# A recurrent scan over 128 steps: exponentials issued a step ahead, expert tiles spread over three steps, and four extra bf16 matrices ahead of each step's spreads

## The chip, the cores and the metric

The kernel runs on one core of a Trainium2 chip. The metric is the time of the whole program on the device in microseconds, as the median over several runs. One core has five engines that run their own instruction streams and meet only at semaphores: TensorE (PE in the profile, with its weight loads as PEld), VectorE (DVE), ScalarE (ACT), GpSimd (POOL) and SyncE (SP), which here only issues DMAs.

## The reference: what is computed

The network has four layers over 4096 tokens of 128 channels. Every layer normalises x, computes a mixer s and a feed-forward part g, and adds s * silu(g) to x. The change lies in layer 2, whose mixer is a selective scan (Mamba) and whose feed-forward part picks 2 of 16 experts for each token:

```python
xz = xn @ W_in;  xi, z = split(xz)
xc = silu(causal_conv(xi) + conv_b)
dt_lo, Bm, Cm = split(xc @ W_xp)
delta = softplus(dt_lo @ W_dt + dt_bias);  A = -exp(A_log)
def step(h, inp):                        # 256 channels x 16 states
    dA = exp(dt_t[..., None] * A)
    h = h * dA + (dt_t * u_t)[..., None] * B_t[:, None, :]
    return h, einsum('bdn,bn->bd', h, C_t)
y = (ys + xc * D_skip) * silu(z);  s = y @ W_out + x

h = relu(tensor @ W1[e] + b1[e]);  y = h @ W2[e] + b2[e]   # experts, 512 hidden
```

Each of 16 sequences has 256 tokens; the reference writes the layers for smaller batches and the kernel applies them to all.

## The kernel before, in words

Layers 0 and 1 run first in one loop over 8 chunks of 512 tokens (two sequences), then `layer2_route` normalises, routes the tokens to experts and scatters them into sorted rows, then `layer2_mix` does the scan and the experts, then layer 3 runs in a loop. Only `layer2_mix` and the layout of one weight array are touched.

`layer2_mix` is written out without a loop: CHUNKS = 8 chunks of 512 tokens, each with PAIRS = 16 steps, 128 steps in all. With k the chunk, n the step in it and g = 16k + n, one step handles 16 of the 256 inner channels as two groups of 8 channels x 16 states, so each group fills 128 partitions. What a step does:

- PE `spread_pairs` (L1094): four fp32 matrices of 32 rows by 512 columns. Two copy the rows of delta (`DL`) for step g + 1 into banks 0 and 1 of the PSUM, two copy delta * u (`DU`) for step g into banks 2 and 3. It waits for ACT's exponentials of step g (`decay_ready`), which read banks 0 and 1, and for DVE's product of step g - 1 (`drive_done`), which reads banks 2 and 3. The four lie on different rows of the array and run together; an fp32 matrix is two instructions in the trace.
- ACT `decay` (L1253): two exponentials, `DA`, double buffered.
- DVE `drive`: the product with B (L1337, `DB`), then the scan over time (L1343, `ST`).
- POOL (L1398): the product with C.
- PE `add_states` (L1122), every second step: sums over the 16 states.

Beside this, two kinds of work are cut into pieces and attached to steps. `head(k + 1, n)` is one of up to 16 pieces of the next chunk's preparation (layer norm, input projection, convolution, silu, softplus), on PE, ACT and DVE; all PE pieces go through the one PSUM bank `LANE`, so a PE piece waits for the ACT copy of the piece before it. Piece 7 holds both silus with a table load on either side, piece 11 the first part of the softplus, piece 12 its logarithm, again with two table loads. And each chunk has 10 expert tiles of 128 rows (SLOTS), from step FIRST = 5 on: `tile_rows` transposes the rows on PE (L1140), ACT copies them (L1262, `XT`); `tile_hidden` is the first expert matrix on PE (L1145) and four relus on ACT (L1267, `H`); `tile_out` is the second matrix with its bias on PE (L1156, L1157) and a copy on ACT (L1274, `YO`). Step n does rows and hidden of tile j and the output of tile j - 1.

The order on each engine is the order in which the code is written. ACT's order in a step is decay(n), XT, YO, H, head piece n; PE's is spreads, rows, output of j - 1, hidden of j, states, head piece n. SP loads each tile's weights as one transfer of 578 KB, `WB`, and its rows, `XR`, once the output of the tile two before has been computed.

Of the kernel before, what the change touches and what calls it, by code (L numbers as in the profile page):

```python
# [12 lines left out]
D = 128  # L13
# [962 lines left out]
MIX_SEMS = (LN_SEMS + LINKS + "xn_loaded0 xn_loaded1 xn_loaded2 s_stored tile_loaded0 tile_loaded1 tile_stored0 tile_stored1 rows_ready rows_taken hid_ready hid_done out_ready out_taken "  # L976
# [4 lines left out]
FIRST = 5  # L981
PAIRS = DI // 16
RING = 4


def layer2_mix(nc, c, w, wf, r, xn_mid, s_mid, xs_mid, ys_mid, PB):
    with ExitStack() as ctx:
# [5 lines left out]
        xn_loaded, tile_loaded, tile_stored = (s.xn_loaded0, s.xn_loaded1, s.xn_loaded2), (s.tile_loaded0, s.tile_loaded1), (s.tile_stored0, s.tile_stored1)  # L993
        B1 = 2 * HID2
        B2 = B1 + 4
# [5 lines left out]
        with nc.Block() as block:  # L1001
            @block.sync
            def _(sp):
# [38 lines left out]
            def _(pe):  # L1042
# [54 lines left out]
                def spread_pairs(k, n):  # L1097
# [35 lines left out]
                def tile_rows(j):  # L1133
                    k = j // SLOTS
                    pe.wait_ge(tile_loaded[j % 2], 32 * (j // 2 + 1))
# [12 lines left out]
                def tile_out(j):  # L1148
                    k = j // SLOTS
                    pe.wait_ge(s.hid_done, 4 * j + 4)  # L1150
                    if j:
                        pe.wait_ge(s.out_taken, j)
                    if j % SLOTS == 0 and k + 1 < CHUNKS:
                        pe.wait_ge(s.xm_ready, k + 2)
                    for i in range(4):
                        nc.tensor.matmul(PB[:, SMALL, 0:128], b.H[:, i, :], b.WB[:, j % 2, HID2 + i * 128:HID2 + (i + 1) * 128], start=i == 0, stop=False)  # L1156
# [29 lines left out]
            def _(act):  # L1186
# [58 lines left out]
                def decay(k, n):  # L1245
                    g = PAIRS * k + n
                    h, i, strip = place(n)
# [10 lines left out]
                def tile_rows(j):  # L1258
# [3 lines left out]
                    nc.scalar.activation(b.XT[:], PB[:, WORK, 0:128], ACT.Copy).then_inc(s.rows_taken, 1)  # L1262
# [13 lines left out]
                for step in range(PAIRS):  # L1276
                    head(0, step)
                for k in range(CHUNKS):
                    for n in range(PAIRS):
                        decay(k, n)  # L1280
                        j = SLOTS * k + n - FIRST
                        if FIRST <= n < FIRST + SLOTS:
                            tile_rows(j)
                        if FIRST < n <= FIRST + SLOTS:
                            tile_out(j - 1)
                        if FIRST <= n < FIRST + SLOTS:
                            tile_hidden(j)
# [760 lines left out]
def layouts(i):  # L2048
# [22 lines left out]
    w2f = np.concatenate([i["L2_ffn_W1"], i["L2_ffn_W2"].reshape(E2, 4, 128, D).transpose(0, 2, 1, 3).reshape(E2, 128, 512),  # L2071
                          i["L2_ffn_b1"].reshape(E2, 4, 128).transpose(0, 2, 1), b2], 2)
# [40 lines left out]
```

## Time and profile before

| what | value |
|---|---|
| median of 3 runs | 4766.21 us (4755.93 to 4780.89) |
| profiled execution, its own time | 4755.87 us |
| its span | 4754.3 us |
| span, granted TensorE clock (mean) | 0.788 |
| PE busy, DVE busy, ACT busy, POOL busy | 3385.2, 2565.2, 1804.2, 1275.9 us |
| steps of `layer2_mix` in the trace | from 1356 to 2450 us |

Busy times are for the whole program; for the change only the stretch of `layer2_mix` counts, some 1090 us of the 4754. In the trace a step begins with the product on DVE (L1337), so the start of one to the start of the next is the length of a step. The granted clock is a share of full speed: 0.5 is 1.2 GHz and 1.0 is 2.4 GHz, and a mean in between says how the stretch was divided between the two. The start to start distances of the 8 chunks are 135.6, 144.4, 139.0, 140.9, 138.9, 140.0 and 144.4 us for chunks 0 to 6, and 96.1 us for the last, which has no next chunk to prepare; its steps 6 to 13 take 61.4 us of that. The page gives 3.4 us from issue to landing for a tile's weights and 3.6 us for its rows (medians of 80 each).

### The profile page before, as it was taken

What the parts mean: (1) busy time and instruction counts of PE and PEld (TensorE: products, weight loads), DVE (VectorE), ACT (ScalarE), POOL (GpSimd) and SP (SyncE); (2) the same over time, 40 slices, a digit from 0 to 9 for tenths busy, and PEclk for the clock granted to TensorE, in tenths of its full rate; (3) what the DMA queues carried; (4) which work ended last, traced back from release to release, by engine and by line L of the source; (5) the groups of instructions that cost most, each with busy time, mean ns of one, the idle gap of its engine ahead of it and who ended that gap; (6) DMA issues with size and microseconds to landing.
All of it is one profiled execution on the core that took longest, in us unless ns stands there. A gap on an engine that the chain in (4) does not pass through costs nothing. (4 is left out here: it accounts for less than half of the span.)

```text
span 4754.3 us, 51362 instructions
## 1 busy us (share of the span) xinstructions
PE 3385.2 (71%) x18378; PEld 1798.5 (38%) x18378; DVE 2565.2 (54%) x3680; ACT 1804.2 (38%) x3620; POOL 1275.9 (27%) x991
## 2 busy tenths in 40 slices
PE   6888888882357666666667868687686777868677
PEld 3444444441223333333333434343343433434343
DVE  3444444443645455555546656665565656656665
ACT  3333333332233343333323434344343443434344
POOL 0000000003412222322225334242442425334242
PEclk8888888885566676767677979888786887968888
DMA  1000000002211221111120000000000000000000
GB/s 81 7 7 7 7 7 7 7 7 89 74 33 49 66 64 50 60 53 47 54 68 1 5 8 5 8 2 6 5 5 8 5 8 1 5 8 5 8 2 6
DMA packets 70675, 111.70 MB, mean 23 GB/s; under 512 B 8640, under 2 KB 46016, under 8 KB 69952
## 3 DMA queue, kind: packets, MB, share of 16 engines
q1 hardware_dynamic: 65088, 97.85, 6.4%
q0 software_dynamic: 5376, 11.02, 0.9%
q8 instruction: 135, 2.21, 0.2%
q14 instruction: 76, 0.62, 0.0%
HBM read 82.09 MB, written 26.74 MB: 23 GB/s over the span
## 5 line engine op out<-in xcount | busy, mean ns | idle before, releaser
L1398 POOL TENSOR_TENSOR l_ST<-l_ST,l_CT 128x1024 f32<-128x1024 f32 x128 | 303.9, 2375 | 770.0 <-DVE l_ST L1343 770.0
L369 ACT ACTIVATE l_PT<-PB 128x512 f32<-128x512 f32 x512 | 277.9, 594 | 521.2 <-PE PB L280 521.2
L280 PE MATMUL PB<-l_QM,l_KP 32*128 32x256 f32 x2048 | 356.3, 476 | 131.7 <-DVE l_QM L418 76.0
L1094 PE MATMUL PB<-l_DL,consts 32*128 32x512 f32 x512 | 219.7, 938 | 311.3 <-ACT l_DA L1253 297.1
L1337 DVE TENSOR_TENSOR l_DB<-PB,l_BT 128x1024 f32<-128x1024 f32 x128 | 156.5, 1223 | 413.7 <-PE PB L1094 413.7
L407 DVE TENSOR_REDUCE keep_MXP<-PB 128x4 f32<-128x1024 f32 x256 | 301.3, 1218 | 109.8 <-PE PB L253 109.7
L280 PEld LDWEIGHTS PB<-l_QM,l_KP 32*128 32x128 f32 x2048 | 231.5, 233 | 246.6 <-ACT l_PT L369 98.0
L1343 DVE TENSOR_TENSOR_SCAN l_ST<-l_DA,l_DB 128x1024 f32<-128x1024 f32 x128 | 299.4, 2339 | 4.4
L1548 POOL TENSOR_TENSOR l_PT<-l_PT,l_PEN 128x512 f32<-128x512 f32 x168 | 213.4, 1292 | 157.9 <-ACT l_PT L369 157.9
L703 POOL MEMSET l_KV<- 128x4 f32 x8 | 0.8, 105 | 923.0 <-POOLq L109 923.0
L1812 POOL TENSOR_TENSOR l3f_SQ<-l3f_RW 128x512 f32<-128x512 f32 x128 | 147.1, 1149 | 312.7 <-ACT l3f_RW L1678 312.7
L1616 PE MATMUL PB<-l3f_QK 64*64 64x128 f32 x2048 | 168.7, 314 | 80.4 <-DVE l3f_QK L1752 80.4
L1094 PE MATMUL PB<-l_DU,consts 32*128 32x512 f32 x512 | 217.9, 936 | 0.0
L1094 PEld LDWEIGHTS PB<-l_DL,consts 32*128 32x128 f32 x512 | 52.7, 243 | 432.3 <-ACT l_DA L1253 430.1
L253 PE MATMUL PB<-l_KP,l_QP 32*128 32x256 f32 x2048 | 198.6, 516 | 15.6 <-issue 15.6
L1703 ACT ACTIVATE l3f_PP<-PB,l3f_MN 128x128 f32<-128x128 f32 x512 | 146.3, 368 | 163.7 <-DVE l3f_MN L1764 163.7
L1821 POOL TENSOR_TENSOR l3f_PP<-l3f_PP,l3f_RS 128x512 f32<-128x512 f32 x128 | 133.3, 1041 | 257.1 <-DVE l3f_RS L1770 257.1
L294 PE MATMUL PB<-l_PT,keep_VT 128*32 128x256 f32 x2048 | 161.4, 469 | 36.2 <-POOL l_PT L1548 25.6
L1616 PEld LDWEIGHTS PB<-l3f_QK 64*64 64x64 f32 x2048 | 134.4, 157 | 115.0 <-issue 111.8
L1817 POOL TENSOR_TENSOR l3f_C<-l3f_C 128x512 f32<-128x512 f32 x128 | 162.3, 1268 | 48.3 <-DVE l3f_C L1741 48.3
L1253 ACT ACTIVATE l_DA<-PB,keep_aneg 128x510 f32<-128x510 f32 x256 | 161.6, 688 | 33.9 <-PE PB L1094 24.6
L1584 PE MATMUL PB<-l3f_HS,w3fs 128*128 128x512 f32 x256 | 145.9, 654 | 37.1 <-DVE l3f_HS L1720 37.1
(414 smaller groups left out, 7327.6 us busy)
## 6 DMA issues: line engine op xcount, KB each, us to landing
l_WB<-in_w2f_dram SPq DMA_DIRECT2D x80, 578.0 KB, 3.4
l_XR<-xs_mid SPq DMA_DIRECT2D x80, 64.0 KB, 3.6
ys_mid<-l_YO SPq DMA_DIRECT2D x80, 64.0 KB, 3.4
s_mid<-keep_S SPq DMA_DIRECT2D x17, 256.0 KB, 2.0
w3fs<-in_w3f_dram SPq DMA_DIRECT2D x1, 3125.0 KB, 17.3
keep_XI<-in_x_dram SPq DMA_DIRECT2D x9, 256.0 KB, 3.2
x_mid<-keep_X SPq DMA_DIRECT2D x9, 256.0 KB, 3.2
keep_SI<-s_mid SPq DMA_DIRECT2D x9, 256.0 KB, 2.7
```

The lines of the kernel that those rows point to most:

```text
L253: last = nc.tensor.matmul(PB[:, r, qt * SEQ:(qt + 1) * SEQ], b.QP[rows, a, q0:q0 + 128], b.KP[rows, a, i, sq * SEQ:(sq + 1) * SEQ], start= ...
L280: last = nc.tensor.matmul(PB[:, 4 + u % STBANKS, kt * SEQ:(kt + 1) * SEQ], b.KP[rows, a, i, k0:k0 + 128], b.QM[rows, n % 2, :], start=True ...
L294: last = nc.tensor.matmul(PB[32 * r:32 * r + 32, 7, 0:SEQ], VT[:, 2 * sq + kt, 8 * a + 2 * r + i, :], b.PT[:, (NR * (2 * j + i) + r) % PSL ...
L369: nc.scalar.activation(b.PT[:, u % PSLOTS].rearrange("p k q -> p (k q)"), PB[:, 4 + u % STBANKS, :], ACT.Exp).then_inc(s.exp_done, 1)
L407: nc.vector.tensor_reduce(dst[:, 2 * pair:2 * pair + 2, :, 16 + n % 2], PB[:, 2 * pair:2 * pair + 2, :].rearrange("p r (t k) -> p r t k", ...
L1094: return nc.tensor.matmul(PB[:, bank + e, :], c.rowsel[q:q + 32, i * 128:(i + 1) * 128], src[q:q + 32, k % 2, h, :], start=True, stop=True)
L1253: last = nc.scalar.activation(b.DA[:, g % 2, e, :].rearrange("p (s t) -> p s t", t=SEQ)[:, :, 1:SEQ], PB[:, e, :].rearrange("p (s t) -> p ...
L1343: nc.vector.tensor_tensor_scan(b.ST[:, g % RING].rearrange("p k t -> p (k t)"), b.DA[:, g % 2].rearrange("p k t -> p (k t)"), b.DB[:, g % ...
L1398: nc.gpsimd.tensor_tensor(b.ST[:, g % RING], b.ST[:, g % RING], b.CT[:, k % 2, :].unsqueeze(1).broadcast_to([128, 2, T]), ALU.mult).then_i ...
L1548: nc.gpsimd.tensor_tensor(pt, pt, b.PEN[:, 2 * sq:2 * sq + 2, :], ALU.mult).then_inc(s.weighed_pool, 1)
L1616: nc.tensor.matmul(PB[r, k, win * 128:win * 128 + 2 * WIN], b.QK[r, hp, q0:q0 + WIN], b.QK[r, NT + hp, k0:k0 + 2 * WIN], start=win == 0, s ...
L1817: nc.gpsimd.tensor_tensor(b.C1[:, v % 2, :], b.C1[:, v % 2, :], b.C2[:, v % 2, :], ALU.add).then_inc(s.rot_summed, 1)
```

## The change

Four things change in `layer2_mix`.

1. ACT issues `decay(g + 1)` in step g instead of `decay(g)`, behind the output copy of a tile and ahead of the head piece and the relus. ACT's head pieces come one step later (piece n - 1 in step n), and so do DVE's pieces 11 and 12 of the softplus (now 12 and 13).
2. A tile now lies over three steps: rows of j, hidden of j - 1, output of j - 2, in the order output, hidden, states, rows on PE; FIRST is 4 instead of 5. The transposed rows go to the bank `SMALL`, which the outputs also use, instead of `WORK`.
3. Before each step's spreads, behind their waits, PE runs FILL = 4 bf16 matrices of 128 x 512 on constants into a bank that the spreads then overwrite. Their result is not used.
4. SP loads a tile in three transfers (rows, first matrix with its bias, second matrix with its bias), each with its own wait, and the weight array is laid out so that each part is contiguous.

```diff
-FIRST = 5
+FIRST = 4
+FILL = 4
@@ load_tile (SP)
+                    if j >= 2:
+                        sp.wait_ge(s.rows_ready, j - 1)
+                    sp.dma_start(b.XR[:, j % 2, :], xs_mid[bass.ds(row, 128), :]).then_inc(rows_loaded[j % 2], 16)
+                    matrices = wf[bass.ds(bank, 1), :, :].rearrange("e p f -> p (e f)")
+                    if j >= 2:
+                        sp.wait_ge(s.hid_done, 4 * (j - 1))
+                    sp.dma_start(b.WB[:, j % 2, 0:V2], matrices[:, 0:V2]).then_inc(first_loaded[j % 2], 16)
+                    if j >= 2:
+                        sp.wait_ge(s.out_ready, j - 1)
+                    sp.dma_start(b.WB[:, j % 2, V2:W2ROW], matrices[:, V2:W2ROW]).then_inc(second_loaded[j % 2], 16)
@@ spread_pairs (PE), behind its waits
+                    for _ in range(FILL):
+                        nc.tensor.matmul(PB[:, PAIR0, :], c.identb, c.windowb, start=True, stop=True)
@@ the pieces of a step (PE)
-                        if FIRST <= n < FIRST + SLOTS:
-                            tile_rows(j)
-                        if FIRST < n <= FIRST + SLOTS:
-                            tile_out(j - 1)
-                        if FIRST <= n < FIRST + SLOTS:
-                            tile_hidden(j)
+                        if FIRST + 2 <= n < FIRST + 2 + SLOTS:
+                            tile_out(j - 2)
+                        if FIRST + 1 <= n < FIRST + 1 + SLOTS:
+                            tile_hidden(j - 1)
...
+                        if FIRST <= n < FIRST + SLOTS:
+                            tile_rows(j)
@@ the pieces of a step (ACT)
+                decay(0)
                 for k in range(CHUNKS):
                     for n in range(PAIRS):
-                        decay(k, n)
                         j = SLOTS * k + n - FIRST
+                        if FIRST + 2 <= n < FIRST + 2 + SLOTS:
+                            tile_out(j - 2)
+                        if PAIRS * k + n + 1 < PAIRS * CHUNKS:
+                            decay(PAIRS * k + n + 1)
+                        if n and k + 1 < CHUNKS:
+                            head(k + 1, n - 1)
+                        if FIRST + 1 <= n < FIRST + 1 + SLOTS:
+                            tile_hidden(j - 1)
                         if FIRST <= n < FIRST + SLOTS:
                             tile_rows(j)
-                        if FIRST < n <= FIRST + SLOTS:
-                            tile_out(j - 1)
-                        if FIRST <= n < FIRST + SLOTS:
-                            tile_hidden(j)
-                        if k + 1 < CHUNKS:
-                            head(k + 1, n)
```

How this stands on the engines. First PE, a step in the middle of a chunk's tiles with one head piece (step 6 of a chunk). Before:

```order
L1094 MATMUL PB<-l_DL,consts 128x512
L1094 MATMUL PB<-l_DU,consts 128x512
L1094 MATMUL PB<-l_DL,consts 128x512
L1094 MATMUL PB<-l_DU,consts 128x512
L1140 MATMUL PB<-consts,l_XR 128x128
L1156 MATMUL PB<-l_WB,l_H 128x128 x4
L1157 MATMUL PB<-l_WB,consts 128x128
L1145 MATMUL PB<-l_XT,l_WB 128x128 x4
L1068 MATMUL PB<-l_XM,w2s 128x512
```

Spreads, rows (L1140), output of the tile before (L1156, L1157), hidden (L1145), head piece (L1068). The same step after:

```order
L1119 MATMUL PB<-windowb,identb 128x512 x4
L1103 MATMUL PB<-l_DL,consts 128x512
L1103 MATMUL PB<-l_DU,consts 128x512
L1103 MATMUL PB<-l_DL,consts 128x512
L1103 MATMUL PB<-l_DU,consts 128x512
L1173 MATMUL PB<-l_WB,l_H 128x128 x4
L1174 MATMUL PB<-l_WB,consts 128x128
L1162 MATMUL PB<-l_XT,l_WB 128x128 x4
L1151 MATMUL PB<-consts,l_XR 128x128
L1077 MATMUL PB<-l_XM,w2s 128x512
```

Four matrices on constants (L1119) stand ahead of the spreads, and the rows (L1151) have moved behind output and hidden. Second ACT, where the two silus are: steps 7 and 8 of a chunk before.

```order
L1253 ACTIVATE l_DA<-PB,keep_aneg 128x2x255 x2
L1262 ACTIVATE l_XT<-PB 128x128
L1274 ACTIVATE l_YO<-PB 128x128
L1267 ACTIVATE l_H<-PB,l_WB 128x128 x4
L1215 ACT_TABLE_LOAD
L1215 ACTIVATE l_ZS<-l_ZS 128x1024
L1218 ACTIVATE l_XC<-l_XC 128x512 x2
L1219 ACT_TABLE_LOAD
L1253 ACTIVATE l_DA<-PB,keep_aneg 128x2x255 x2
L1262 ACTIVATE l_XT<-PB 128x128
```

The exponentials of step 8 (the second L1253 row) stand behind the silus and their table loads. After, step 8 of a chunk and the start of step 9:

```order
L1290 ACTIVATE l_YO<-PB 128x128
L1269 ACTIVATE l_DA<-PB,keep_aneg 128x2x255 x2
L1232 ACT_TABLE_LOAD
L1232 ACTIVATE l_ZS<-l_ZS 128x1024
L1235 ACTIVATE l_XC<-l_XC 128x512 x2
L1236 ACT_TABLE_LOAD
L1283 ACTIVATE l_H<-PB,l_WB 128x128 x4
L1278 ACTIVATE l_XT<-PB 128x128
L1290 ACTIVATE l_YO<-PB 128x128
L1269 ACTIVATE l_DA<-PB,keep_aneg 128x2x255 x2
```

The exponentials of step 9 (the first L1269 row) now stand ahead of the silus, and the relus and the copy of the rows (L1283, L1278) behind them.

## Rows read from the trace of the kernel before

**Rows 1.** Stretches by engine: busy us (count) of PE, PEld, DVE, ACT, POOL, clock, DMA.
```profile
1782.10:1923.00 140.90, 98.10 (x411) 47.08 (x410) 76.89 (x52) 54.58 (x115) 41.21 (x18) 0.69 0.19 56
...
2346.30:2442.40 96.10, 67.86 (x356) 35.37 (x356) 61.06 (x34) 33.22 (x88) 33.26 (x16) 0.79 0.24 70
```

**Rows 2.** Waits summed over 1365 to 2445 us: us, times, longest.
```profile
PE PB L1094 <- ACT l_DA L1253: 296.3, 113, 6.4
...
PEld PB L1140 <- DMA l_XR<-xs_mid: 36.4, 26, 1.9
```

**Rows 3.** Timeline, DVE products, chunk 3: start us, us, engine, line, operation, idle before.
```profile
1782.06 1.23 DVE L1337 TENSOR_TENSOR l_DB<-PB,l_BT 128x1024 f32<-128x1024 f32 x1 [1.16 <-PE PB L1094]
...
1826.32 1.22 DVE L1337 TENSOR_TENSOR l_DB<-PB,l_BT 128x1024 f32<-128x1024 f32 x1
...
1832.26 1.22 DVE L1337 TENSOR_TENSOR l_DB<-PB,l_BT 128x1024 f32<-128x1024 f32 x1 [2.40 <-PE PB L1094]
...
1846.54 1.23 DVE L1337 TENSOR_TENSOR l_DB<-PB,l_BT 128x1024 f32<-128x1024 f32 x1 [10.73 <-PE PB L1094]
...
1864.87 1.22 DVE L1337 TENSOR_TENSOR l_DB<-PB,l_BT 128x1024 f32<-128x1024 f32 x1 [5.47 <-PE PB L1094]
...
1872.59 1.23 DVE L1337 TENSOR_TENSOR l_DB<-PB,l_BT 128x1024 f32<-128x1024 f32 x1 [3.53 <-PE PB L1094]
...
1885.33 1.23 DVE L1337 TENSOR_TENSOR l_DB<-PB,l_BT 128x1024 f32<-128x1024 f32 x1 [2.25 <-PE PB L1094]
...
1909.04 1.22 DVE L1337 TENSOR_TENSOR l_DB<-PB,l_BT 128x1024 f32<-128x1024 f32 x1 [7.69 <-PE PB L1094]
...
1923.01 1.22 DVE L1337 TENSOR_TENSOR l_DB<-PB,l_BT 128x1024 f32<-128x1024 f32 x1 [2.12 <-PE PB L1094]
```

**Rows 4.** Timeline of PE, chunk 3, at the lower clock.
```profile
1844.23 1.22 PE L1094 MATMUL PB<-l_DL,consts 32*128 32x512 f32 x1 [5.49 <-ACT l_DA L1253]
...
1846.52 1.91 PE L1156 MATMUL PB<-l_WB,l_H 128*128 128x128 f32 x8
...
1834.80 2.08 PE L1145 MATMUL PB<-l_XT,l_WB 128*128 128x128 f32 x8
...
1836.81 1.94 PE L1122 MATMUL PB<-l_ST,consts 128*32 128x512 f32 x8
```

**Rows 5.** Timeline of PE, chunk 3, at the higher clock.
```profile
1863.52 0.69 PE L1094 MATMUL PB<-l_DL,consts 32*128 32x512 f32 x1 [1.83 <-ACT l_DA L1253]
...
1864.75 1.06 PE L1156 MATMUL PB<-l_WB,l_H 128*128 128x128 f32 x8
...
1866.15 1.16 PE L1145 MATMUL PB<-l_XT,l_WB 128*128 128x128 f32 x8
...
1867.24 1.12 PE L1081 MATMUL PB<-l_BC,w2s 32*128 32x512 f32 x2
```

**Rows 6.** Timeline of PE, eight bf16 matrices on constants (layer 3), both clocks.
```profile
2477.95 3.56 PE L127 MATMUL PB<-windowb,identb 128*128 128x512 bf16 x8
...
2646.71 1.89 PE L127 MATMUL PB<-windowb,identb 128*128 128x512 bf16 x8
```

**Rows 7.** Timeline of ACT, chunk 3.
```profile
1834.91 0.28 ACT L1274 ACTIVATE l_YO<-PB 128x128 f32<-128x128 f32 x1 [1.94 <-PE PB L1157]
...
1836.91 1.14 ACT L1267 ACTIVATE l_H<-PB,l_WB 128x128 f32<-128x128 f32 x4 [1.73 <-PE PB L1145]
...
1838.08 1.28 ACT L1215 ACT_TABLE_LOAD   x1
...
1842.92 1.26 ACT L1253 ACTIVATE l_DA<-PB,keep_aneg 128x510 f32<-128x510 f32 x2
...
1890.03 1.28 ACT L1233 ACT_TABLE_LOAD   x1
...
1893.69 0.60 ACT L1240 ACTIVATE l_BT<-PB 128x512 f32<-128x512 f32 x1
```

**Rows 8.** Groups by line, 1365 to 2445 us: busy us, mean ns | idle before.
```profile
L1343 DVE TENSOR_TENSOR_SCAN l_ST<-l_DA,l_DB 128x1024 f32<-128x1024 f32 x128 | 299.4, 2339 | 4.4
```

More of the change, by code:

```diff
@@ L992, in layer2_mix @@
         SO = c.S
-        xn_loaded, tile_loaded, tile_stored = (s.xn_loaded0, s.xn_loaded1, s.xn_loaded2), (s.tile_loaded0, s.tile_loaded1), (s.tile_stored0, s.tile_stored1)
-        B1 = 2 * HID2
-        B2 = B1 + 4
+        xn_loaded, tile_stored = (s.xn_loaded0, s.xn_loaded1, s.xn_loaded2), (s.tile_stored0, s.tile_stored1)
+        rows_loaded, first_loaded, second_loaded = (s.rows_loaded0, s.rows_loaded1), (s.first_loaded0, s.first_loaded1), (s.second_loaded0, s.second_loaded1)
+        B1 = HID2
+        V2 = B1 + 4
+        B2 = V2 + HID2
         PAIR0, WORK, SMALL, LANE, SUMS = 2, 5, 6, 7, 4
@@ L1134, in tile_rows, with tile_hidden @@
                     k = j // SLOTS
-                    pe.wait_ge(tile_loaded[j % 2], 32 * (j // 2 + 1))
+                    pe.wait_ge(rows_loaded[j % 2], 16 * (j // 2 + 1))
+                    if j >= 2:
+                        pe.wait_ge(s.out_taken, j - 1)
+                    if j % SLOTS == 0 and k + 1 < CHUNKS:
+                        pe.wait_ge(s.xm_ready, k + 2)
+                    nc.tensor.transpose(PB[:, SMALL, 0:128], b.XR[:, j % 2, :], c.ident).then_inc(s.rows_ready, 1)
+                def tile_hidden(j):
+                    k = j // SLOTS
+                    pe.wait_ge(s.rows_taken, j + 1)
+                    pe.wait_ge(first_loaded[j % 2], 16 * (j // 2 + 1))
                     if j:
@@ L1148, in tile_out @@
                 def tile_out(j):
-                    k = j // SLOTS
                     pe.wait_ge(s.hid_done, 4 * j + 4)
+                    pe.wait_ge(second_loaded[j % 2], 16 * (j // 2 + 1))
+                    if j % SLOTS < SLOTS - 1:
+                        pe.wait_ge(s.rows_taken, j + 2)
                     if j:
                         pe.wait_ge(s.out_taken, j)
-                    if j % SLOTS == 0 and k + 1 < CHUNKS:
-                        pe.wait_ge(s.xm_ready, k + 2)
                     for i in range(4):
-                        nc.tensor.matmul(PB[:, SMALL, 0:128], b.H[:, i, :], b.WB[:, j % 2, HID2 + i * 128:HID2 + (i + 1) * 128], start=i == 0, stop=False)
+                        nc.tensor.matmul(PB[:, SMALL, 0:128], b.H[:, i, :], b.WB[:, j % 2, V2 + i * 128:V2 + (i + 1) * 128], start=i == 0, stop=False)
                     nc.tensor.matmul(PB[:, SMALL, 0:128], c.ones[0:1, :], b.WB[0:1, j % 2, B2:B2 + 128], start=False, stop=True).then_inc(s.out_ready, 1)
@@ L1243, in head, with decay @@
                         nc.scalar.activation(b.CT[:, p, :], PB[:, LANE, :], ACT.Copy).then_inc(s.c_copied, 1)
-                def decay(k, n):
-                    g = PAIRS * k + n
-                    h, i, strip = place(n)
+                def decay(g):
+                    h, i, strip = place(g % PAIRS)
                     if g >= 2:
@@ L1261, in tile_rows @@
                         act.wait_ge(s.hid_ready, j)
-                    nc.scalar.activation(b.XT[:], PB[:, WORK, 0:128], ACT.Copy).then_inc(s.rows_taken, 1)
+                    nc.scalar.activation(b.XT[:], PB[:, SMALL, 0:128], ACT.Copy).then_inc(s.rows_taken, 1)
                 def tile_hidden(j):
@@ L1320, in head @@
                         last.then_inc(s.conv_done, 1)
-                    elif step == 11:
+                    elif step == 12:
                         dve.wait_ge(s.dt_u, k + 1)
                         nc.vector.scalar_tensor_tensor(out=b.EE[:], in0=b.UU[:], scalar=-1.0, in1=b.EE[:], op0=ALU.add, op1=ALU.subtract).then_inc(s.dt_error, 1)
-                    elif step == 12:
+                    elif step == 13:
                         dve.wait_ge(s.dt_log, k + 1)
@@ L2070, in layouts @@
     b2[:, 0] = i["L2_ffn_b2"]
-    w2f = np.concatenate([i["L2_ffn_W1"], i["L2_ffn_W2"].reshape(E2, 4, 128, D).transpose(0, 2, 1, 3).reshape(E2, 128, 512),
-                          i["L2_ffn_b1"].reshape(E2, 4, 128).transpose(0, 2, 1), b2], 2)
+    w2f = np.concatenate([i["L2_ffn_W1"], i["L2_ffn_b1"].reshape(E2, 4, 128).transpose(0, 2, 1),
+                          i["L2_ffn_W2"].reshape(E2, 4, 128, D).transpose(0, 2, 1, 3).reshape(E2, 128, 512), b2], 2)
     w3 = dict(q=head_pairs(i["L3_attn_Wq"]), k=head_pairs(i["L3_attn_Wk"]), v=i["L3_attn_Wv"], bv=rep(i["L3_attn_bv"]),
```

9 lines of the change are left out of this document (1 added, 8 removed).

## The prediction, made before the changed kernel was run

> **What bounds the kernel now.** I first asked the windows for the stretch of the scan. Chunk 3 takes 140.9 us; PE is busy for 98.1 of it, DVE for 76.9, ACT for 54.6, POOL for 41.2, at a mean granted clock of 0.69 [rows 1]. No engine is full, so the chunk is bound by a ring of waits. The waits name the ring: PE's spreads waited 296 us for ACT's exponentials, in 113 of the 128 steps [rows 2], and DVE's product in turn stands idle before nearly every step, up to 10.73 us [rows 3]. The reader is to see in code order why: ACT's exponentials of step n + 1 stand last in a queue behind the copy of the rows, the output copy, the relus and the head piece of step n, and each of these waits for PE work that itself stands behind the spreads. So a tile step is one chain, PE and ACT taking turns, and PE rests some 1.8 to 2.4 us in it, and 5.49 us where the silus are [rows 4, 5]. PE then runs at the lower of its two levels for much of the time.
>
> The timeline gives chunk 3 by pieces (start of one product to the start of another) [rows 3]: steps 0 to 5 44.3 us, step 6 5.9, step 7 14.3 (silus), steps 8 and 9 18.3, step 10 7.7, step 11 12.7, steps 12 and 13 23.7 (logarithm), steps 14 and 15 14.0. The sum is 140.9.
>
> **Prices.** At the higher level: the spreads hold PE for about 1.1 us (1863.52 to the output at 1864.75, less the transpose), an output with its bias 1.4 (1864.75 to 1866.15), a hidden part 1.1 (to 1867.24), a head matrix 1.1 [rows 5]. At the lower level: spreads 2.1, output 1.91 and its bias 0.7, hidden 2.0 (1834.80 to 1836.81), sums of states 1.94 every second step [rows 4]; a head matrix I put at 2.0 and the sums at the higher level at 1.0, by the same factor. ACT: output copy 0.28, two exponentials 1.26, four relus 1.14, a copy out of the PSUM 0.60, the silus with their loads 1838.08 to 1842.92, that is 4.84, the logarithm piece 1890.03 to 1894.29, that is 4.26 [rows 7]. Handing over from one engine to the next costs about 0.1 (an estimate: the spreads' start at 1863.52 to the product at 1864.87 is 1.35 us [rows 3, 5], of which they take some 1.25 to their end).
>
> The new matrices: eight of this very form took 1.89 us at the higher and 3.56 us at the lower level [rows 6]. Half of it, less some of the tail that the spreads overlap, is 0.86 and 1.7 us a step. Over 128 steps that is 110 or 218 us of PE time that did not exist, so this part pays only if it is hidden or raises the clock.
>
> **The change by steps.** In the new order ACT needs only spreads, output and output copy before it can start the next exponentials. A tile step without a head piece at the higher level: fill 0.86, spreads 1.1, output 1.4, copy 0.28, exponentials 1.26, hand-overs 0.3: 5.2 us. With a head piece the ACT copy (0.6) comes behind the exponentials and PE's head matrix (1.1) behind that, since both use one bank: 6.8 us. PE's own sum is nearly the same (0.86 + 1.1 + 1.4 + 1.1 + 0.5 + 0.3 + 1.1 = 6.4), so PE is close to full there. At the lower level the sum is 1.7 + 2.1 + 2.6 + 2.0 + 0.5 + 2.0 = 10.9, and 12.7 with states.
>
> - Steps 0 to 5. DVE is the bound in steps 2, 4 and 5 (10.4, 8.2, 8.2 us in all chunks; step 6 begins with no idle time [rows 3]) and keeps its work. No step can be shorter than product and scan, 1.22 + 2.34 = 3.6 us [rows 3, 8]. Steps 0, 1 and 3 are chains: 3.6 + 5.2 + 4.5 at the higher level, 5.8 + 7.8 + 6.0 at the lower. Sum 40.4 or 47.1. DVE's part holds PE idle, so I take a mostly low clock: 44.
> - Step 6. PE did its part while DVE was still in step 5: 3.6 or 7.5. I take 5.5. Step 7: 5.2 or 10.7; I take 6.
> - Steps 8 and 9. The exponentials now pass ahead of the silus, but the relus do not: in step 8 they end at 5.2 + 4.84 + 1.14, and the row copy at about 11.4, and the output of step 9 waits for it. From there output 1.4, hidden 1.1, states 1.0, transpose 0.3, head piece 9 (four instructions) 1.9: 17.1 for both, 23.5 at the lower level. PE rests 4 us before, so I add most of a cold restart: 19.5. The stall of step 7 is gone, and this is what is late next.
> - Step 10: 6.8 or 10.8, I take 7. Step 11: 6.8 or 12.7, I take 7.5.
> - Steps 12 and 13. The spread of B (head piece 13) waits for the copy that ends the logarithm piece, and this now lies in step 13 itself. Step 12 takes 6.8; in it ACT has 3.3 us of softplus behind its copy, so relus and row copy end at 10.4, step 13's output at 11.9, its exponentials at 13.5, the logarithm piece at 17.7, the head matrix at 18.8. Lower level 25.1. Taken: 21. DVE waits for the softplus too, but has caught up before.
> - Steps 14 and 15: 10.5 or 16.6. PE rests about 1.5 of each 5.2, so I take 12.5.
>
> Sum: 44 + 5.5 + 6 + 19.5 + 7 + 7.5 + 21 + 12.5 = 123.0 us; all at the higher level 109.3, all at the lower 154.0. My value lies 0.3 of the way up from the higher end, since steps 6, 7, 10 and 11 have PE almost without a rest and the trace has the slow spreads behind a rest of 5.49 us and quick ones behind a rest of 1.83 us [rows 4, 5].
>
> Chunks 1 to 6 average 141.3 us, so 18.3 x 6 = 110 us. Chunk 0, 135.6 us, has no sums of a chunk before: 13. The last chunk has no head pieces; its steps 6 to 13 take 61.4 of its 96.1 us (given with the profile) and come to 8 x 6 = 48, and steps 4 and 5 lose nothing: 12. Together 135 us.
>
> The three transfers cost nothing. They are issued some 7 us or more before the step that uses them, against 3.4 to 3.6 us to landing. The old wait for rows, 36.4 us in 26 of the 80 tiles and at most 1.9 us in one [rows 2], stood in the chain and is inside the lengths above. If the cover is gone it stays, at most 36 us in all.
>
> 4755.9 - 135 = 4620.9 for a profiled execution. The median shown is 10.3 us above the profiled execution's own 4755.87, so I predict 4631.
>
> **The clock, by trace and by rule.** In chunk 3 PE was busy 0.70 of the time and got 0.69; in the last chunk 0.71 and 0.79 [rows 1], so the same busy share can get different clocks. The Trainium skill, page TensorE: Matmul & The Clock Gate, section A second HAM failure mode: psum-queue depth-cycling, says that small rests between groups of matrices can by themselves keep the clock going up and down, and that throughput suffers from the repeated change. By that rule fills that stand behind the wait, as here, lengthen the busy part and leave the rest where it is, and the clock would keep its present share: the first rival below. Chunk 3, with both levels in one stretch, agrees with the rule as far as it goes.
>
> **Rivals.**
> - The clock keeps its present share. The rests remain in steps 2 to 5, 9, 13 to 15; against it, the tile steps have hardly any. At 0.69 the lower level holds 0.6 of the time: 109.3 + 0.6 x 44.7 = 136.1 a chunk, 5 us less than now, 31 us over six chunks and about 10 in the others: 4725.
> - The clock stays high nearly throughout. For: PE gets 0.86 to 1.7 us more to do in every step. Against: rests of 4 us remain in steps 9 and 13. 109.3 a chunk: 192 + 20 + 17 = 229 us less, 4537.
> - Slower: the fills run at the lower level on the ring. Place: every tile step; there PE is the bound when slow (10.9 to 12.7 us), of which 1.7 are fills, which before it did not have. A chunk comes to 141 as now when the lower level holds 0.71 of the time (141 - 109.3 = 0.71 x 44.7), a granted clock of 0.65; below that the change loses. At the end of it 154.0: 76 + 31 us more, 4873. Against: both levels occur in this stretch as it is [rows 4, 5], and PE will rest less.
> - The change does not act: something in ACT's queue (the output copy that waits for PE) keeps the exponentials as late as before, and what is won goes into the fills. By code order the copy waits only 1.4 us of PE work, so this is small: 4766.
>
> **Numbers.** Forecast 0.50 (its own range 4585 to 4690), present clock 0.19, high clock 0.15, slower 0.10, no effect 0.06. The range reaches from near the high clock to past the present clock: 4540 to 4765. About 0.5% (24 us) is what a measurement can tell from no change. Faster takes the first three less the part of the second that comes within 24 us: 0.82. Same 0.08, slower 0.10.
>
> **What would show it.** Right: spreads no longer wait hundreds of us for the exponentials; a chunk near 123 us and mean clock near 0.8 in the stretch; step 7 near 6 us; in step 9 the output waits for the copy of the rows, in step 13 the head matrix for the copy of B; steps 2, 4 and 5 unchanged; fills mostly 0.86 us a step. Wrong: a clock at or below 0.69, PE waiting for `WB` or `XR`, or steps 12 and 13 longer than 23.7 us together.

## The result, and the profile after

| | before | after |
|---|---|---|
| median | 4765.16 us | 4600.63 us (4 runs, 4553.26 to 4605.71) |
| after / before | | 0.963, 95% interval 0.956 to 0.970 |
| profiled execution, its own time and span | 4755.87, 4754.3 us | 4605.71, 4604.1 us |
| first product of the scan to the last | 1079.2 us | 890.5 us |
| layer 3 loop, to the end of the span | 2277.2 us | 2318.5 us |

The change is faster by 3.7%; 4631 was forecast. The scan won 189 us of its 1079, more than the 135 forecast, and layer 3, which the change does not touch, took 41 us more in this execution. All ratios here and below leave out runs more than 1.5% above the fastest of their kernel (one each of e1 and e3), while the medians hold them.

The windows for a chunk in the middle and for the last one (engines' busy time with counts, then granted clock, DMA share, GB/s), against [rows 1]:

```profile
1825.80:1941.80 116.00, 91.19 (x468) 42.51 (x474) 79.92 (x52) 52.09 (x116) 40.40 (x18) 0.90 0.24 68
...
2173.80:2252.00 78.20, 67.96 (x410) 34.30 (x418) 62.08 (x34) 32.34 (x89) 34.56 (x16) 0.96 0.29 79
```

A chunk fell from 140.9 to 116.0 us and the last from 96.1 to 78.2. The clock rose from 0.69 to 0.90. PE is busy for 91 us of a chunk as against 98, although it now runs 64 more matrices, since more of the work runs at the higher clock. The waits over the whole scan, before and after (PEld is the loading of a matrix's weights, which stands ahead of it):

```profile
PEld PB L1094 <- ACT l_DA L1253: 427.8, 125, 7.3
DVE l_DB L1337 <- PE PB L1094: 407.4, 102, 11.4
```

```profile
DVE l_DB L1355 <- PE PB L1103: 226.0, 74, 12.3
...
PEld PB L1119 <- ACT l_DA L1269: 54.5, 42, 3.2
...
PE PB L1119 <- ACT l_DA L1269: 16.9, 26, 2.4
```

The first instruction of a step on PE is now the constant matrix (L1119). It waits for ACT's exponentials for 17 us in all, where the spreads waited 296 us [rows 2], and its weight loads for 55 us, where they waited 428. DVE's waits for the spreads fell from 407 us to 226. The starts of DVE's product through one chunk, to be laid beside [rows 3]:

```profile
1825.79 1.22 DVE L1355 TENSOR_TENSOR l_DB<-PB,l_BT 128x1024 f32<-128x1024 f32 x1 [1.61 <-PE PB L1103]
...
1866.47 1.22 DVE L1355 TENSOR_TENSOR l_DB<-PB,l_BT 128x1024 f32<-128x1024 f32 x1
...
1870.15 1.23 DVE L1355 TENSOR_TENSOR l_DB<-PB,l_BT 128x1024 f32<-128x1024 f32 x1
...
1875.93 1.23 DVE L1355 TENSOR_TENSOR l_DB<-PB,l_BT 128x1024 f32<-128x1024 f32 x1 [1.33 <-PE PB L1103]
...
1881.06 1.22 DVE L1355 TENSOR_TENSOR l_DB<-PB,l_BT 128x1024 f32<-128x1024 f32 x1 [1.58 <-PE PB L1103]
...
1896.67 1.22 DVE L1355 TENSOR_TENSOR l_DB<-PB,l_BT 128x1024 f32<-128x1024 f32 x1 [12.06 <-PE PB L1103]
...
1903.33 1.23 DVE L1355 TENSOR_TENSOR l_DB<-PB,l_BT 128x1024 f32<-128x1024 f32 x1 [2.47 <-PE PB L1103]
...
1910.27 1.23 DVE L1355 TENSOR_TENSOR l_DB<-PB,l_BT 128x1024 f32<-128x1024 f32 x1 [3.39 <-PE PB L1103]
...
1931.56 1.23 DVE L1355 TENSOR_TENSOR l_DB<-PB,l_BT 128x1024 f32<-128x1024 f32 x1 [5.12 <-PE PB L1103]
...
1941.84 1.23 DVE L1355 TENSOR_TENSOR l_DB<-PB,l_BT 128x1024 f32<-128x1024 f32 x1 [1.61 <-PE PB L1103]
```

| steps | before | taken in the prediction | after |
|---|---|---|---|
| 0 to 5 | 44.3 | 44 | 40.7 |
| 6 | 5.9 | 5.5 | 3.7 |
| 7 | 14.3 | 6 | 5.8 |
| 8 and 9 | 18.3 | 19.5 | 20.7 |
| 10 | 7.7 | 7 | 6.7 |
| 11 | 12.7 | 7.5 | 6.9 |
| 12 and 13 | 23.7 | 21 | 21.3 |
| 14 and 15 | 14.0 | 12.5 | 10.3 |

The prediction had steps 2, 4 and 5 unchanged. Over chunks 1 to 6, steps 2 and 4 took 11.0 and 8.8 us instead of 10.4 and 8.2: the scan on DVE takes 2.86 and 2.83 us in these two steps of the chunk above, as against 2.29 alone, which the last section comes back to.

The new wait in step 9 is where it was expected. (The table has one chunk, before and after; by the means of chunks 1 to 6, steps 8 and 9 went from 20.2 to 20.6.) The ACT timeline shows the silus with their loads, and behind them relus and row copy:

```profile
1878.70 1.28 ACT L1232 ACT_TABLE_LOAD   x1
...
1883.54 1.14 ACT L1283 ACTIVATE l_H<-PB,l_WB 128x128 f32<-128x128 f32 x4
...
1884.56 0.29 ACT L1278 ACTIVATE l_XT<-PB 128x128 f32<-128x128 f32 x1
```

and PE's output part rests 4.26 us for that copy and then runs cold, that is at the lower clock (1.16 us becomes 2.08 for the hidden part), until the next constants at the higher clock. In step 13 the spread of B (L1097) rests for the copy behind the logarithm, also as expected:

```profile
1885.11 2.04 PE L1173 MATMUL PB<-l_WB,l_H 128*128 128x128 f32 x8 [4.26 <-ACT l_XT L1278]
...
1887.80 2.08 PE L1162 MATMUL PB<-l_XT,l_WB 128*128 128x128 f32 x8
...
1894.36 1.03 PE L1119 MATMUL PB<-windowb,identb 128*128 128x512 bf16 x4
...
1925.74 2.07 PE L1097 MATMUL PB<-l_BC,consts 32*128 32x512 f32 x2 [3.45 <-ACT l_BT L1257]
```

Four constants at the lower and at the higher level, for comparison with [rows 6]:

```profile
1859.62 1.87 PE L1119 MATMUL PB<-windowb,identb 128*128 128x512 bf16 x4 [2.55 <-DVE l_DB L1355]
...
1873.62 1.03 PE L1119 MATMUL PB<-windowb,identb 128*128 128x512 bf16 x4
```

They take 1.79 us (to the spreads at 1861.41) or 0.95 us (to 1874.57) of PE's time; 1.7 and 0.86 were worked out. Half of the eight matrices in [rows 6] is 1.78 and 0.95, so the tail that the prediction took off for an overlap was not there.

### The profile page after: what moved, and what is told of

Read it like the earlier page. It is cut to its first block and busy times, and to the rows that moved or that the text cites. A ratio compares the mean times of both kernels' runs of the same rounds, so it can differ in the third digit from the quotient of the medians.

```text
span 4604.1 us, 52632 instructions
## 1 busy us (share of the span) xinstructions
PE 3359.9 (73%) x18738; PEld 1785.4 (39%) x18890; DVE 2584.6 (56%) x3680; ACT 1783.8 (39%) x3620; POOL 1274.1 (28%) x991
## 5 line engine op out<-in xcount | busy, mean ns | idle before, releaser
L280 PE MATMUL PB<-l_QM,l_KP 32*128 32x256 f32 x2048 | 392.9, 517 | 131.7 <-DVE l_QM L418 76.0
L280 PEld LDWEIGHTS PB<-l_QM,l_KP 32*128 32x128 f32 x2048 | 251.9, 254 | 263.8 <-ACT l_PT L369 101.2
L1361 DVE TENSOR_TENSOR_SCAN l_ST<-l_DA,l_DB 128x1024 f32<-128x1024 f32 x128 | 317.2, 2478 | 4.4
L1269 ACT ACTIVATE l_DA<-PB,keep_aneg 128x510 f32<-128x510 f32 x256 | 161.1, 683 | 177.1 <-DVE l_ST L1361 92.5
L253 PE MATMUL PB<-l_KP,l_QP 32*128 32x256 f32 x2048 | 208.9, 539 | 15.6 <-issue 15.6
L418 DVE TENSOR_TENSOR l_QM<-l_QP,PB 128x256 f32<-128x256 f32 x128 | 53.8, 420 | 272.0 <-PE PB L262 268.5
L294 PE MATMUL PB<-l_PT,keep_VT 128*32 128x256 f32 x2048 | 180.6, 513 | 33.6 <-POOL l_PT L1566 16.0
L1119 PE MATMUL PB<-windowb,identb 128*128 128x512 bf16 x456 | 133.6, 414 | 61.0 <-DVE l_DB L1355 37.9
L1770 DVE TENSOR_TENSOR l3f_QK<-l3f_C,l3f_RN 128x512 f32<-128x512 f32 x128 | 149.7, 1169 | 26.5 <-DVE l3f_NR L1763 24.1
```

What stands on the lines that cost most here:

```text
L253: last = nc.tensor.matmul(PB[:, r, qt * SEQ:(qt + 1) * SEQ], b.QP[rows, a, q0:q0 + 128], b.KP[rows, a, i, sq * SEQ:(sq + 1) * SEQ], start= ...
L280: last = nc.tensor.matmul(PB[:, 4 + u % STBANKS, kt * SEQ:(kt + 1) * SEQ], b.KP[rows, a, i, k0:k0 + 128], b.QM[rows, n % 2, :], start=True ...
L294: last = nc.tensor.matmul(PB[32 * r:32 * r + 32, 7, 0:SEQ], VT[:, 2 * sq + kt, 8 * a + 2 * r + i, :], b.PT[:, (NR * (2 * j + i) + r) % PSL ...
L1269: last = nc.scalar.activation(b.DA[:, g % 2, e, :].rearrange("p (s t) -> p s t", t=SEQ)[:, :, 1:SEQ], PB[:, e, :].rearrange("p (s t) -> p ...
L1361: nc.vector.tensor_tensor_scan(b.ST[:, g % RING].rearrange("p k t -> p (k t)"), b.DA[:, g % 2].rearrange("p k t -> p (k t)"), b.DB[:, g % ...
```

## The experiments

Three theories were set against each other. A, the prediction's: the exponentials leaving the chain bring the gain, and the constant matrices pay for themselves through the clock. B: the matrices bring it. C: the order brings it, and the matrices are a net cost.

The best measure of the scan is the distance from its first product to its last, since the stages around it vary by more than some of the edits bring. It comes from one profiled execution per version. Two versions were profiled twice, and their scans differ by 2.4 and 3.2 us, so a difference of a few us between scans tells nothing. All runs in one table; the chunk is the mean of chunks 1 to 6, the ratio is to the kernel before on the same chip. A granted clock of 0.5 and 1.0 are the two levels, 1.2 and 2.4 GHz.

| run | median us | ratio (95%) | scan us | chunk | last chunk | clock, chunks 1 to 6 |
|---|---|---|---|---|---|---|
| before | 4765 | 1 | 1079.2 | 141.3 | 96.1 | 0.70 |
| after | 4600.6 | 0.963 (0.956 to 0.970) | 890.5 | 116.1 | 78.2 | 0.90 |
| e1_fill0 | 4537.7 | 0.949 (0.943 to 0.954) | 859.0 | 112.6 | 72.1 | 0.73 |
| e2_before_fill4 | 4799.2 | 1.006 (1.001 to 1.010) | 1103.5 | 143.4 | 98.9 | 0.86 |
| e3_before_ahead | 4573.5 | 0.955 (0.948 to 0.962) | 865.8 | 110.3 | 94.9 | 0.78 |
| e4_after_late | 4693.7 | 0.984 (0.979 to 0.989) | 1007.4 | 129.7 | 100.0 | 0.84 |
| e6_fill8 | 4663.5 | 0.976 (0.968 to 0.983) | 945.4 | 122.9 | 86.9 | 0.94 |
| e7_one_wait | 4550.1 | 0.954 (0.946 to 0.961) | 861.6 | 112.4 | 74.7 | 0.77 |
| e8_fill_rest9 | 4518.1 | 0.949 (0.943 to 0.955) | 832.3 | 109.2 | 72.1 | 0.80 |
| e5_long_behind | 4485.2 | 0.943 (0.936 to 0.950) | 785.5 | 101.8 | 72.1 | 0.85 |
| e9_after_again | 4575.0 | 0.960 (0.955 to 0.965) | 888.1 | 116.0 | 78.2 | 0.91 |
| e10_best_again | 4475.4 | 0.940 (0.936 to 0.944) | 782.3 | 102.1 | 71.1 | 0.84 |

**e1_fill0: the change without the matrices.**

```diff
-FILL = 4
+FILL = 0
```

> The changed kernel without its four bf16 matrices per step. Theory A (the gain comes from the exponentials leaving the chain, the matrices pay for themselves by a higher clock): granted clock in the scan falls from 0.90 to about 0.75, a chunk stays near 116 us, total 4590 to 4640. Theory B (the matrices carry the gain through the clock): a chunk goes back above 130 us, total 4710 or more. Theory C (the order carries it and the matrices are a net cost of up to 0.86 us in each step that PE bounds): a chunk near 103 us, total 4500 to 4540.

```profile
1505.70:2181.60 675.90, 540.78 (x2460) 271.43 (x2458) 480.96 (x313) 314.23 (x691) 242.36 (x103) 0.73 0.25 69
```

(Stretch of chunks 1 to 6.) The clock fell back to 0.73, as theory A said, but the scan did not stay: it got 31.5 us shorter, and the whole 1.5% faster (0.949 against 0.963, and 0.960 in the repeat). The profiled execution was the longest of e1's four, 4574.98 us, but not by its scan: all of its chunks from 1 to 6 take 112.6 or 112.7 us, as most of e7's do, which also has no matrices. The expectation of a break-even, mine, was wrong. The chunk moved by only 3.5 us, so theory C's full 0.86 us a step is wrong as well, though its range for the total holds: the matrices give most of their time back and not all of it. They do not give it back in step 9, where PE works cold behind its rest with them or without them (output, hidden part and sums of states, as in the rows of the change above); that step takes 15.5 us with and 15.0 without. Without them:

```profile
1903.66 2.04 PE L1173 MATMUL PB<-l_WB,l_H 128*128 128x128 f32 x8 [5.23 <-ACT l_XT L1278]
...
1906.36 2.08 PE L1162 MATMUL PB<-l_XT,l_WB 128*128 128x128 f32 x8
...
1908.36 1.94 PE L1133 MATMUL PB<-l_ST,consts 128*32 128x512 f32 x8
```

They do give it back in steps 1 and 14, which take 5.0 and 5.2 us with them and 6.2 and 6.6 without. Output and hidden part of step 14, without the matrices and with them:

```profile
1945.31 2.08 PE L1173 MATMUL PB<-l_WB,l_H 128*128 128x128 f32 x8
...
1948.04 2.08 PE L1162 MATMUL PB<-l_XT,l_WB 128*128 128x128 f32 x8
```

```profile
1931.26 1.16 PE L1173 MATMUL PB<-l_WB,l_H 128*128 128x128 f32 x8
...
1932.77 1.16 PE L1162 MATMUL PB<-l_XT,l_WB 128*128 128x128 f32 x8
```

In steps 8, 10, 11 and 15 they cost 0.9 to 1.2 us each.

**e2_before_fill4: only the matrices.**

```diff
+                    for _ in range(FILL):
+                        nc.tensor.matmul(PB[:, PAIR0, :], c.identb, c.windowb, start=True, stop=True)
                     for e in range(2):
```

> The kernel before with only the four bf16 matrices added ahead of each step's spreads. A: the ring of waits is as long as before, 0.86 us longer a step but with a higher clock; the two about cancel: 4730 to 4780, chunk 137 to 142 us. B: most of the gain of the change, 4600 to 4650. C: slower by some 110 us, 4850 to 4880.

```profile
1527.30:2387.40 860.10, 589.88 (x2844) 261.88 (x2843) 462.34 (x312) 328.01 (x691) 241.84 (x103) 0.86 0.18 54
```

```profile
PE PB L1111 <- ACT l_DA L1256: 242.0, 90, 6.4
```

The clock rose from 0.70 to 0.86 and the scan got 24 us longer. Theory B fails: the waits for the exponentials are all still there. The row is of chunks 1 to 6 alone, 242 us in 90 steps, and the same stretch before has 237 us in 87. The run is a shade slower than A's range (4799 for at most 4780), and in its sense.

**e3_before_ahead: only the exponentials ahead.**

```diff
+                decay(0)
                 for k in range(CHUNKS):
                     for n in range(PAIRS):
-                        decay(k, n)
                         j = SLOTS * k + n - FIRST
                         if FIRST <= n < FIRST + SLOTS:
                             tile_rows(j)
                         if FIRST < n <= FIRST + SLOTS:
                             tile_out(j - 1)
+                        if PAIRS * k + n + 1 < PAIRS * CHUNKS:
+                            decay(PAIRS * k + n + 1)
```

> The kernel before with only ACT's exponentials of step g + 1 moved ahead of the relus and the head piece of step g (tiles stay in two steps, no added matrices, one transfer). A: a tile step's chain becomes spreads 1.1, transpose 0.3, copy 0.3, output 1.4, copy 0.3, exponentials 1.3, so 5 to 6.5 us at the higher clock; the silus no longer hold up the spreads; 4600 to 4680. B: little, 4720 to 4770. C: 4500 to 4600.

```profile
1465.20:2127.10 661.90, 517.77 (x2460) 262.91 (x2458) 510.09 (x313) 323.24 (x690) 263.85 (x102) 0.78 0.23 71
```

Moving this one block gives 213 us of the scan, more than the whole change (189). At 4573.5 it lies below A's range and inside C's. So with the exponentials early, all the rest of the reordering (tiles over three steps, head pieces a step later, three transfers) is worth little: e1, which has it, has a scan only 6.8 us shorter than e3, and the intervals of their totals overlap. It wins 22.8 us in the last chunk, which in e3 stays near its old length (94.9 us), and loses 2.3 us in each of chunks 1 to 6. The waits name what is late in e3:

```profile
PEld PB L1140 <- DMA l_XR<-xs_mid: 109.7, 54, 4.0
```

With the quicker steps the rows of a tile, issued behind its 578 KB of weights after the output of the tile two before, come late, up to 4 us. Before, this was 36 us [rows 2].

**e4_after_late: the change with the exponentials back.**

```diff
-                decay(0)
                 for k in range(CHUNKS):
                     for n in range(PAIRS):
+                        decay(PAIRS * k + n)
...
-                        if PAIRS * k + n + 1 < PAIRS * CHUNKS:
-                            decay(PAIRS * k + n + 1)
```

> The changed kernel with ACT's exponentials of step g back at the start of step g (three-step tiles, four matrices and three transfers stay). A: relus, row copy, head piece and silus are back in the chain: a chunk of 130 to 138 us, total 4700 to 4770. B: as the changed kernel, 4600 to 4630. C: slower than before, 4780 or more.

```profile
1483.40:2261.70 778.30, 589.50 (x2844) 266.79 (x2843) 488.83 (x313) 319.72 (x691) 242.39 (x102) 0.84 0.22 60
```

The scan is 117 us longer than with the change, at a clock of 0.84 as against 0.90, and step 8, with the silus back in the chain, takes 13.1 us. Chunk and total (129.7 and 4694) lie just below A's range. The rest of the change (tiles over three steps, head pieces a step later, three transfers) is worth 96 us where the exponentials are late: 1007.4 against 1103.5 for e2, both with the matrices. Between e3 and e1, where they are early, it was 7. Its three parts were not tested one by one, but for the waits of the transfers (e7).

**e6_fill8: eight matrices.**

```diff
-FILL = 4
+FILL = 8
```

> The changed kernel with eight matrices per step instead of four. The fill costs its time and the clock is already at 0.90, so there is less to win from the second four: a chunk rises from 116.1 by 8 to 12 us (four matrices are 0.86 us; PE bounds 10 to 13 of 16 steps), the last chunk from 78.2 to about 90; total 4680 to 4710. Rival, that PE's rests take the fills in: chunk 116 to 119, total 4600 to 4630.

```profile
1507.90:2245.10 737.20, 612.37 (x3180) 287.59 (x3226) 463.35 (x313) 313.00 (x691) 242.53 (x102) 0.94 0.24 64
```

The second four cost 55 us of scan (890.5 to 945.4), the first four 31.5. That is a little below the ranges given for the chunk (122.9 for 124 to 128) and the total (4663.5 for 4680 to 4710). Steps 2, 4 and 5, bound by DVE, did take the matrices in (10.4, 8.3, 8.2 us). The clock rose only from 0.90 to 0.94.

**e8_fill_rest9: matrices only where PE rests.**

```diff
                         spread_pairs(k, n)
+                        if k + 1 < CHUNKS and n == 9:
+                            pe.wait_ge(s.z_copied, 2 * k + 4)
+                            for _ in range(16):
+                                nc.tensor.matmul(PB[:, LANE, :], c.identb, c.windowb, start=True, stop=True)
```

> The changed kernel without the four matrices per step, and in step 9 of a chunk 16 of them (3.4 us at the higher clock) between the spreads and the output, where PE rests 5.2 us for the row copy, into a free bank. If matrices help where PE rests and only cost where it does not, output, hidden, states and head piece 9 run at the higher clock and step 9 falls from 15.0 us to 12 to 13, a chunk from 112.6 to about 110; total 4510 to 4530. Rival: the clock gives nothing because ACT bounds the step: step 9 stays at 15, 4535 to 4545.

```profile
1624.65 3.40 PE L1187 MATMUL PB<-windowb,identb 128*128 128x512 bf16 x15 [0.16 <-issue]
...
1629.73 1.13 PE L1173 MATMUL PB<-l_WB,l_H 128*128 128x128 f32 x8 [1.67 <-ACT l_XT L1282]
...
1631.20 1.16 PE L1162 MATMUL PB<-l_XT,l_WB 128*128 128x128 f32 x8
...
1632.29 1.06 PE L1133 MATMUL PB<-l_ST,consts 128*32 128x512 f32 x8
```

Here the matrices fill the rest itself, and output, hidden part and sums run at 1.13, 1.16 and 1.06 us, where e1 has 2.04, 2.08 and 1.94; step 9 fell from 15.0 to 12.0 us as expected. Chunks 1 to 6 gain 3.4 us each, the scan 26.7 (of which some 6 lie in chunk 0, which varies). The ratios of e8 and e1 to the kernel before are both 0.949, so the gain is shown in the scan and not in the total. So the higher clock is worth having where PE is the bound behind a rest, and the matrices put into that rest cost nothing.

**e7_one_wait: one wait for all three transfers.**

```diff
                     if j >= 2:
-                        sp.wait_ge(s.rows_ready, j - 1)
+                        sp.wait_ge(s.out_ready, j - 1)
                     sp.dma_start(b.XR[:, j % 2, :], xs_mid[bass.ds(row, 128), :]).then_inc(rows_loaded[j % 2], 16)
...
-                    if j >= 2:
-                        sp.wait_ge(s.hid_done, 4 * (j - 1))
...
-                    if j >= 2:
-                        sp.wait_ge(s.out_ready, j - 1)
```

> The changed kernel without the four matrices and with the three transfers of a tile issued together behind the one wait for the output of the tile two before. Theory: the rows and the first matrix are then issued at most one step later and still have a step or more to land: no change, 4525 to 4550. Rival: the separate waits are what keeps the rows from coming late, PE waits for rows by 1 us a tile: 4580 to 4620.

```profile
PEld PB L1147 <- DMA l_XR<-xs_mid: 49.2, 49, 1.9
```

The rows now come late 49 times, which in the change and in e1 does not happen once, but chunks 1 to 6 are no longer than e1's (112.4 for 112.6), so there the waits lie in time that PE has. The last chunk is 2.6 us longer, the scan 861.6 against 859.0. The total, 4550, is at the top of the range of no change, and no difference from e1 can be told.

**e5_long_behind: the long ACT pieces behind the tile work.** No matrices, and

```diff
-                        if n and k + 1 < CHUNKS:
+                        if n and n != 8 and k + 1 < CHUNKS:
                             head(k + 1, n - 1)
                         if FIRST + 1 <= n < FIRST + 1 + SLOTS:
                             tile_hidden(j - 1)
                         if FIRST <= n < FIRST + SLOTS:
                             tile_rows(j)
+                        if n == 8 and k + 1 < CHUNKS:
+                            head(k + 1, n - 1)
+                        if n == 12 and k + 1 < CHUNKS:
+                            softplus_start(k + 1)
```

where `softplus_start` is the three long passes (abs, exp, add) of piece 11, which otherwise stays in place.

> The changed kernel without the four matrices, and on ACT the silus (step 8) and the three long passes of the softplus (step 12) behind the relus and the row copy of their step instead of ahead. If the rest of PE in steps 9 and 13 is the wait for the row copy behind these pieces, as the prediction says, steps 8 and 9 together fall from 19.2 us to 14 to 16, steps 12 and 13 from 20.5 to 18 to 20, and the total is 25 to 45 us below the kernel without the matrices (4537): 4495 to 4515. Rival: ACT's own sum of work bounds these steps, so nothing is won: 4530 to 4545.

```profile
1457.10:2067.90 610.80, 478.12 (x2460) 238.99 (x2458) 504.64 (x312) 310.98 (x691) 247.88 (x103) 0.85 0.28 77
```

ACT in step 8, relus and row copy first, then the load for the silus; and the output part on PE, which rests 0.26 us where it rested 4.26:

```profile
1816.15 1.16 ACT L1285 ACTIVATE l_H<-PB,l_WB 128x128 f32<-128x128 f32 x4
...
1817.15 0.32 ACT L1280 ACTIVATE l_XT<-PB 128x128 f32<-128x128 f32 x1
...
1817.49 1.28 ACT L1239 ACT_TABLE_LOAD   x1
```

```profile
1817.72 1.13 PE L1173 MATMUL PB<-l_WB,l_H 128*128 128x128 f32 x8 [0.26 <-ACT l_XT L1280]
```

Steps 8 and 9 take 12.5 us, steps 12 and 13 17.2, the scan 785.5: 73.5 us less than e1 and 105 less than the change. The total, 4485, is below the 4495 to 4515 expected. The stall that the prediction named as next is real and was worth more than I gave it. PE also stays at the higher clock behind the shorter rest: the output part above takes 1.13 us where e1 has 2.04, and the clock is 0.85 with no constants at all. Step 13 still has its rest for the copy of B, 4.2 us on the mean; this edit does not touch it.

**e9_after_again and e10_best_again.** No edit: the changed kernel, and e5's.

> The changed kernel once more, unaltered, for its layer 3: in the first profile the layer 3 loop took 2318 us against 2277 before, with iterations of 283 to 297 us. Theory: which iterations take 283 or 297 us changes from execution to execution, with when the clock happens to fall, and has nothing to do with the change: the scan takes 890 us again, layer 3 anything from 2265 to 2320, most likely not 2318 with the same iterations long. Rival: the change makes layer 3 slower: 2310 to 2325 again, long in the same iterations.

> The version without the matrices and with the long ACT pieces behind the tile work, unaltered, beside the changed kernel on one chip and in more rounds. Scan 786 us, total 4480 to 4510, 90 to 120 us below the changed kernel.

The layer 3 loop before, after, and in the repeat of after:

```profile
2477.10:4754.30 2277.20, 1671.35 (x10096) 896.12 (x10096) 1375.49 (x2086) 943.98 (x1903) 837.58 (x720) 0.83 0.02 5
```

```profile
2285.60:4604.10 2318.50, 1697.53 (x10008) 920.12 (x10096) 1377.41 (x2086) 943.51 (x1903) 834.70 (x720) 0.81 0.02 5
```

```profile
2283.20:4570.90 2287.70, 1686.16 (x10096) 903.04 (x10096) 1377.53 (x2086) 943.57 (x1903) 835.39 (x720) 0.83 0.02 5
```

The same program took 2318.5 us there once and 2287.7 the other time, with the long iterations (up to 297 us as against 283) in other places: in the first the third and the seventh, in the second only the seventh. The scan was 890.5 and 888.1. So 31 of the 41 us that layer 3 took more did not come again with the same program. Whether the change sways it a little is open: over the five profiles with four or eight constants in every step it took 2288 to 2319 us, 2304 on the mean, over the seven without 2266 to 2309, 2286 on the mean. On one chip e9 has 4575.0 us and e10 4475.4: the last version is 2.2% faster than the change and 6.0% faster than the kernel before. Its total is a little below the 4480 to 4510 expected, and the 99.5 us between the two are inside the expected 90 to 120.

## Why the prediction was right, and where it was not

- The bound. A ring of waits through ACT's queue: shown. The block of exponentials alone moves 213 us (e3), and taking it back out of the change costs 117 (e4). What the prediction did not see is that this one of the four parts is enough: e3 alone is as fast as all four together or faster (0.955 as against 0.963, intervals overlapping).
- The steps. Seven of the eight pieces came out within 2.5 us of what was taken, and the lengths worked out for the higher clock (40.4, 3.6, 5.2, 17.1, 6.8, 6.8, 18.8, 10.5, together 109.3) are within 0.7 us of the measured ones but for steps 8 and 9 and 12 and 13, in which PE works cold behind its rests. (The terms given for steps 0 to 5 add up to 40.1 and 46.4, not to 40.4 and 47.1; it changes nothing.) The sum of 123.0 was 7 us high. The mis-sized term is how far each piece lies between the lengths at the two clocks: 0.3 of the way up was taken, 0.15 was measured (116.1 - 109.3 over 44.7), at a granted clock of 0.90. In the last chunk 8 x 6 = 48 us was taken for steps 6 to 13; they took 43.5.
- From the scan to the total. 189 us were won there as against 135, and 150 in the profiled execution, since layer 3 ran 41 us longer in it. That the median came as near as 30 us to the forecast is in part luck: the scan was 54 us better than forecast, and layer 3 took most of that back.
- What is late next. The row copy behind the silus in step 9 and the copy of B in step 13: both rests are in the rows above. That the row copies cost time is shown by e5; the rest for B was not tested.
- The matrices. The prediction left open which part of the gain they bring. They take 0.95 to 1.79 us of PE in each step and raise the clock from 0.73 to 0.90, and on balance lose 31.5 us of scan (e1; theory C's sign, and in the chunk 3.5 us of the 13 that it gave). No rival said so: all of them priced the change whole, and the rival of the present clock even gave e1's state of PE as the worse one, at 136 us a chunk. With a clock of 0.73 and no matrices it is 112.6, and e7 has the same chunk at 0.77. The step that fails there is that a mean clock of 0.7 was taken to mean slow work on the chain in 0.6 of every step. That the slow stretches of e1 lie largely where DVE or ACT is the bound anyway is what I take from it, and not shown; step 9, the one that was tested (e8), is one where slow work did cost time, and steps 1 and 14 are others.
- The clock rule. The rests stayed and the clock still rose with the constants (e2: from 0.70 to 0.86, with 242 us of waits in chunks 1 to 6 as against 237), so the first rival, that the clock keeps its present share, fails. The Trainium skill's remark in TensorE: Matmul & The Clock Gate, A second HAM failure mode: psum-queue depth-cycling, that small rests can make the clock go up and down, still agrees with e2, whose clock of 0.86 is a mix of both levels; it says nothing of the share, and the share is what the rival had wrong.
- The transfers. No wait for rows or weights is left. By e7 the separate waits are worth nothing that can be told. In e3, with the rows issued behind the whole of the weights and tiles over two steps, the rows come late for 110 us; which of the two would cure that was not tested.

## What to carry to other kernels

Where engines take turns at one another through in-order queues, put first in each queue what another engine's next start depends on, and long pieces that nobody waits for soon behind the short ones that somebody does; that was worth 213 and 73 us here. A higher granted clock is no gain by itself: work added to raise it, put on the chain behind a wait, cost more than it gave with four matrices and with eight, and only the same work put inside a rest ahead of slow work shortened the scan. Test the parts of a bundled change one by one, since one of them can pay for another.

## What the runs showed of the hardware

DVE's scan takes 2.29 us alone. When it starts beside POOL's product it takes longer, mostly up to 3.5 us and 3.61 at most (e3). The quicker versions meet this more often: 3 of the 128 scans took 3.4 us or more before, 2 with the change, 33 in e5 and 38 in e3. In e3, DVE and POOL:

```profile
1789.60 3.43 DVE L1344 TENSOR_TENSOR_SCAN l_ST<-l_DA,l_DB 128x1024 f32<-128x1024 f32 x1
```

```profile
1788.53 2.36 POOL L1399 TENSOR_TENSOR l_ST<-l_ST,l_CT 128x1024 f32<-128x1024 f32 x1
```

The product ends at 1790.89, 1.29 us into the scan, and the scan is 1.14 us longer: it did next to nothing until then. DVE's busy time in the scan stage rose from 598 us before to 617 after and 653 in e5 with the same instructions. The Trainium skill has this in SBUF — State Buffer, in Who interferes with whom: a DVE instruction with two inputs in the SBUF gets its second one through the read port of GpSimd, and the two contend; these rows agree. It may be the next thing to take on, since DVE is busy for 505 of the 611 us of e5's chunks 1 to 6; what it costs the whole was not tested.
